# Delta's input through its 16 ranks: eight column-tiled products, a ScalarE copy and one fp32 product, in a Mamba block between two feed-forward blocks

## The chip, the cores and the metric

The kernel runs on one core of a Trainium2 chip. The metric is the device time of one execution in microseconds (us). TensorE (PE) multiplies, VectorE (DVE), ScalarE (ACT) and GpSimd (POOL) do the elementwise work, and SyncE (SP) issues most of the DMAs. The engines run their own instruction streams in order and meet at semaphores.

## What is computed

The input is 2 sequences of 2048 tokens of 256 numbers. Three layers follow one another, each on a layer-normed input and added back: a gated feed-forward block (hidden width 768, weights stored as integers), a Mamba block (inner width 512, 128 states), and the same feed-forward block again. The change lies in the Mamba block:

```
xz = x @ in_proj_w.T                 # x_in (512), z (512)
xc = causal_conv4(x_in) + conv_b     # per channel
ssm = xc @ x_proj_w.T                # 16 + 128 + 128 columns
dt_r, Bm, _ = split(ssm, [16, 144])
delta = clip(softplus(dt_r @ dt_proj_w.T + dt_proj_b), 0.001, 0.1)
A_bar = exp(delta * A);  B_bar = (A_bar - 1) / A * Bm
h[t] = A_bar[t] * h[t-1] + B_bar[t]
y = h @ C_proj_w.T + xc * D
out = (y * silu(z)) @ out_proj_w.T
```

Delta is a 128-wide quantity that comes from a 16-wide one (`dt_r`).

## The kernel before

**Tiles and halves.** A tile is 512 tokens of one sequence. The two sequences alternate: there are eight *halves* h = 0 to 7, and half h works on the Mamba block (part B) of one tile while it does the first feed-forward block (part A) of the tile that comes next and the second feed-forward block (part C) of the tile that has just left. Half 0 is the start (no C; it is woven with the preparation of the weights), halves 1 to 6 are alike, half 7 has no A, and a last C follows it alone. Activations are laid out with channels on partitions and 512 tokens along the free axis, so that most products are 128x128 weights against 128x512.

**Products.** Operands in half precision come as a high and a low part: for an fp32 accuracy product, three matmuls per 128 input channels (high x high, low weight x high, high weight x low). `ix`/`iz` are the in-projection, `xp0` and `xp1` the products that give delta's input and Bm, `cp` the state-to-channel product, `out` the out-projection, `gate`/`up`/`down` the feed-forward block. For `xp0` the kernel before folds `dt_proj_w @ x_proj_w[0:16]` once, in the preparation (`fill dt0`, a 16-row fp32 product, then `fill t0`, which transposes it), so that `xp0` is a 128-wide product like `xp1`: 12 matmuls each.

**Order and banks.** PE's order is written out by hand: `FIRST` for the preparation and half 0, `ORDER` for halves 1 to 6, `FINAL` for the rest. The order of ACT, DVE and POOL is that of their `half()` functions. Products go to a ring of four PSUM banks `q`: a product waits for whoever read the product four places earlier (`READER`). `down` and `out` use two other banks (`dp`).

**The way of delta.** `xp0` fills a bank; DVE adds the bias (`delta_in`, tile `sp`); ACT loads another function table and takes exp and log (`softplus_exp`, `softplus_log`); DVE clips (`dl`); ACT does `decay_relu` and `decay_exp` and loads the Silu table back; DVE runs a short series, multiplies, adds Bm (`input_in`, an ACT copy of `xp1`'s bank into `bm`) and scans (`hs`). `cp0` waits for the scan.

In halves 1 to 6 ACT comes to this after `split_hi`, two copies of the next A input (`xs<-xn`); the second one waits for DVE's `normalize(g, "A", (2, 3))`, which stands behind `hidden(g, "C", (4, 5))`, the reader of `up5`. In PE's order `up5` is just ahead of `xp0`.

Of the kernel before, what the change touches and what calls it, by code (L numbers as in the profile page):

```python
# [24 lines left out]
P = 128  # L25
# [11 lines left out]
TAPS = 4  # L37
EPS = 1e-5
# [19 lines left out]
def has(part, h):  # L58
# [54 lines left out]
def plan():  # L113
# [10 lines left out]
    for what, part, h in (*FIRST, *middle, *FINAL):  # L124
# [17 lines left out]
        elif what[:-1] == "xp":  # L142
            reader[take("ring", what + part, h)] = ("pc", h + 1) if what == "xp0" else ("bm", h + 1)
        elif what[:-1] in ("ix", "iz", "cp"):
            reader[take("ring", what + part, h)] = (what[:-1], IC * h + int(what[-1]) + 1)
# [48 lines left out]
def macaron(nc, x, in_w, conv_w, conv_b, xp_w, dt_w, dt_b, a_log, d_skip, c_w, out_w, wg, wu, wd, out):  # L194
    with ExitStack() as ctx:
# [53 lines left out]
        WXH = [sb(f"wxh{n}", [P, IC, N], F16) for n in range(2)]  # L249
        WXL = [sb(f"wxl{n}", [P, IC, N], F16) for n in range(2)]  # L250
# [37 lines left out]
        DTN = sb("dtn", [P, RANK])  # L288
        XPD = DL[0:RANK, :]
        DTT = DA[0:RANK, 0:N]  # L290
# [11 lines left out]
        NTS = SZ[0][:, 3, :]  # L302
# [24 lines left out]
        dtt_ready = sem("dtt_ready")  # L327
        small = sem("small")
# [34 lines left out]
        def _(sp):  # L363
# [8 lines left out]
            sp.dma_start(XPD, xp_w[0:RANK, :]).then_inc(ld["dt"], 16)  # L372
            sp.dma_start(DTN[:, :], dt_w).then_inc(ld["dt"], 16)
# [137 lines left out]
        def _(act):  # L511
# [21 lines left out]
            def fill(what):  # L533
# [15 lines left out]
                elif w in "xt":  # L549
                    act.activation(WXH[int(w == "t")][:, :, :].rearrange("p k n -> p (k n)"), bank[:, :], ACT.Copy)\  # L550
# [6 lines left out]
            def copy_rank():  # L557
                act.wait_ge(dt_turned, 1)
                act.activation(DTT, tp[0][0:RANK, 0:N], ACT.Copy).then_inc(dtt_ready, 1)

            def scale_x(n):
# [4 lines left out]
                else:  # L566
                    act.activation(NTS, filled("dt0")[:, :], ACT.Copy, scale=XRS[:, 1:2]).then_inc(w_act, 1)
# [70 lines left out]

            def softplus_exp(g):
                if g.h == 0:  # L640
                    act.wait_ge(unscale_ready, 1)
                act.wait_ge(pc_ready, g.index(1))
                act.activation(SP[:, :], SP[:, :], ACT.Exp, scale=XRI[:, 1:2]).then_inc(ep_ready, 1)
# [5 lines left out]
            def decay_relu(g):  # L649
                if g.h == 0:  # L650
                    act.wait_ge(const_ready, 3)
# [8 lines left out]
            def input_in(g):  # L660
                bank, uses = g.bank("xp1")
# [3 lines left out]
            def half(g):  # L665
# [47 lines left out]
                if B:  # L713
                    act.preload_act_table_set("natural_log_exp_and_others")
# [7 lines left out]
                if B:  # L722
                    input_in(g)
                if A and g.h > 0:
# [82 lines left out]
            silu_z(start, (2,))  # L807
            act.preload_act_table_set("natural_log_exp_and_others")
# [5 lines left out]
            gate(start, "A", (4,))  # L814
            input_in(start)
            gate(start, "A", (5,))
# [32 lines left out]
            hidden_high(late, "C", (4, 5))  # L849
            act.preload_act_table_set("natural_log_exp_and_others")  # L850
# [5 lines left out]
            input_in(late)  # L856
# [11 lines left out]
        def _(dve):  # L868
# [109 lines left out]
            def delta_in(g):  # L978

                bank, uses = g.bank("xp0")  # L980
# [172 lines left out]
            def x_proj_low(n):  # L1153
# [3 lines left out]
                high, low = (w[n][:, :, :].rearrange("p k n -> p (k n)") for w in (WXH, WXL))  # L1157
                dve.tensor_tensor(low, q[at % RING][:, :], high, ALU.subtract).then_inc(w_dve, 1)
# [28 lines left out]
            def x_proj_scale(n):  # L1187
# [4 lines left out]
                else:  # L1192
                    at = NUMBER["ring", "dt0", -1]
# [521 lines left out]
```

## Time and profile before

| | |
|---|---|
| time, 3 runs | 528.2, 530.04, 530.41 us; median 530.04 |
| the profiled execution | 528.34 us, of which 526.5 are its span |
| PE busy | 495.4 us |
| DVE, ACT, POOL busy | 415.4, 279.3, 235.7 us |
| one middle half (start of `xp0` to the next one) | 58.8 us (177.70 to 236.53) |

The span runs from the first to the last instruction; 1.84 us lie around it. A matmul's duration in the trace overlaps that of the next, so the pace of PE is read from the starts. "Idle before" is the time in which an engine had nothing running before an instruction, and after the arrow stands what it waited for.

### The profile page before, as it was taken

To read this page: it belongs to the slowest core of one execution; us is meant where nothing else is said; L and a number is where in the kernel's file an instruction comes from. 1 tells how busy PE (TensorE), PEld (TensorE's weight loads), DVE (VectorE), ACT (ScalarE), POOL (GpSimd) and SP (SyncE) were. 2 spreads that over 40 slices of the span, in tenths; PEclk is the share of its full clock that TensorE was granted. 3 is DMA by queue.
4 is the path that set the end of the run, shared out by engine and by line. 5 is a ranking of instruction groups with operands and counts; after the bars stand their busy time and mean duration, and the time that the engine had idled before them with its cause. 6 is when DMAs were issued, how large, how long until landed. Compare 5 with 4: busy or idle time off the path is not lost.

```text
span 526.5 us, 7720 instructions
## 1 busy us (share of the span) xinstructions
PE 495.4 (94%) x2657; PEld 292.6 (56%) x2657; DVE 415.4 (79%) x841; ACT 279.3 (53%) x472; POOL 235.7 (45%) x216
## 2 busy tenths in 40 slices
PE   2789988999999999999999999999999999999686
PEld 2346436646584457646574556646584557645444
DVE  4888996897879977997879877997879877787442
ACT  5384871477408671577408671577408671575032
POOL 1232237164733737163733735163733737163422
PEclk9898999999999999999999999999999999999979
DMA  8401000002020022003020112002020011000001
GB/s 294 130 0 43 2 0 2 0 2 42 21 61 2 9 34 81 1 1 42 23 60 1 20 23 81 1 2 41 24 60 1 18 26 42 1 1 21 20 1 42
DMA packets 27240, 16.84 MB, mean 32 GB/s; under 512 B 15264, under 2 KB 26528, under 8 KB 27184
## 3 DMA queue, kind: packets, MB, share of 16 engines
q1 hardware_dynamic: 26368, 15.26, 11.3%
q8 instruction: 40, 0.66, 0.5%
q10 hardware_dynamic: 816, 0.79, 0.5%
q14 instruction: 16, 0.13, 0.1%
HBM read 8.71 MB, written 4.19 MB: 24 GB/s over the span
## 4 chain that ended last, share of the span: by engine, by line
PE 81%; DVE 10%; ACT 3%; issue 3%; DMA 1%; POOL 1%; POOLq 0%; SPq 0%; ACTq 0%; DVEq 0%
PE q L1579 53%; PE dp L1579 25%; PE tp L1484 3%; DVE xc L968 1%; DMA hh<-in_L_ffn_w_gate_dram 1%; DVE h L943 1%; DVE xn L911 1%; POOL hl L432 1%; DVE hs L1025 1%; ACT xc L572 1%; DVE x L954 1%; DVE st_A L883 1%; DVE wmx L1063 0%; ACT sg L596 0%; DVE xl L920 0%
## 5 line engine op out<-in xcount | busy, mean ns | idle before, releaser
L432 POOL TENSOR_TENSOR hl<-h,hh 128x512 f16<-128x512 f32 x96 | 122.3, 1288 | 102.1 <-ACT hh L604 101.4
L943 DVE SCALAR_TENSOR_TENSOR h<-sg,hsm,q 128x512 f32<-128x512 f32 x96 | 70.5, 741 | 33.6 <-PE q L1579 21.4
L968 DVE SCALAR_TENSOR_TENSOR xc<-xi,cw,xc 128x512 f32<-128x512 f32 x96 | 87.1, 922 | 5.0 <-ACT xi L622 4.5
L578 ACT ACTIVATE xh<-tp 128x512 f16<-128x512 f32 x36 | 19.9, 609 | 113.2 <-PE tp L1484 113.2
L596 ACT ACTIVATE sg<-q 128x512 f32<-128x512 f32 x96 | 56.7, 591 | 36.7 <-PE q L1579 36.7
L604 ACT ACTIVATE hh<-h 128x512 f16<-128x512 f32 x96 | 60.1, 628 | 28.5 <-DVE h L943 28.2
L439 POOL TENSOR_TENSOR xcl<-xc,xch 128x512 f16<-128x512 f32 x32 | 40.6, 1278 | 51.7 <-ACT xch L629 51.7
L1579 PE MATMUL dp<-wo,yu 128*128 128x256 f32 x256 | 58.5, 380 | 1.5 <-POOL yu L447 1.5
L1579 PE MATMUL dp<-wd,hl 128*128 128x256 bf16 x384 | 53.4, 275 | 1.7 <-POOL hl L432 1.7
L1579 PE MATMUL dp<-wd,hh 128*128 128x256 bf16 x384 | 53.5, 276 | 0.9 <-ACT hh L604 0.9
L1579 PEld LDWEIGHTS dp<-wo,yu 128*128 128x128 f32 x256 | 47.2, 190 | 9.0 <-POOL yu L447 2.7
L1579 PEld LDWEIGHTS dp<-wd,hh 128*128 128x128 f16 x384 | 37.9, 99 | 12.9 <-issue 4.6
L447 POOL TENSOR_TENSOR yu<-yu,sz 128x512 f32<-128x512 f32 x32 | 39.6, 1268 | 8.8 <-DVE yu L1039 8.6
L1579 PEld LDWEIGHTS dp<-wd,hl 128*128 128x128 f16 x384 | 37.8, 99 | 7.1 <-issue 2.6
L1579 PE MATMUL q<-xh,wg 128*128 128x512 f16 x120 | 37.0, 391 | 3.8 <-DVE xl L920 3.1
L614 ACT ACTIVATE xc<-q,cb,rw 128x512 f32<-128x512 f32 x32 | 24.9, 779 | 28.9 <-PE q L1579 28.8
L1579 PE MATMUL q<-xl,wih 128*128 128x512 f16 x128 | 38.2, 379 | 0.0
L1579 PE MATMUL q<-xh,wih 128*128 128x512 f16 x128 | 38.1, 379 | 0.0
L1579 PE MATMUL q<-xh,wil 128*128 128x512 f16 x128 | 38.1, 379 | 0.0
L1579 PE MATMUL q<-xl,wg 128*128 128x512 f16 x120 | 37.2, 391 | 0.0
L1579 PE MATMUL q<-xt,wu 128*128 128x512 f16 x144 | 37.0, 379 | 0.0
L1579 PE MATMUL q<-xt,wg 128*128 128x512 f16 x144 | 37.0, 379 | 0.0
(169 smaller groups left out, 845.1 us busy)
## 6 DMA issues: line engine op xcount, KB each, us to landing
xpre<-in_L_attn_x_dram SPq DMA_DIRECT2D x8, 512.0 KB, 4.6
out_dram<-x SPq DMA_DIRECT2D x16, 256.0 KB, 2.1
xc<-in_L_attn_in_proj_w_dram SPq DMA_DIRECT2D x1, 1024.0 KB, 11.2
hl<-in_L_ffn_w_up_dram ACTq DMA_DIRECT2D x3, 256.0 KB, 6.3
hh<-in_L_ffn_w_gate_dram SPq DMA_DIRECT2D x3, 256.0 KB, 6.9
hh<-in_L_ffn_w_down_dram SPq DMA_DIRECT2D x1, 768.0 KB, 8.5
yu<-n_L_attn_out_proj_w_dram SPq DMA_DIRECT2D x1, 512.0 KB, 3.8
yu<-in_L_attn_x_proj_w_dram SPq DMA_DIRECT2D x1, 256.0 KB, 11.4
```

The costliest lines, as they stand in the source:

```text
L432: pool.tensor_tensor(HL[g.f][:, c, :], H[:, j, :], HH[g.f][:, c, :], ALU.subtract)\
L439: pool.tensor_tensor(XCL[:, m, :], XC[g.b][:, m, :], XCH[:, m, :], ALU.subtract)\
L447: pool.tensor_tensor(YU[g.b][:, m, :], YU[g.b][:, m, :], SZ[g.b][:, m, :], ALU.mult)\
L572: act.activation(NIS[:, c, :], NI[:, c, :], ACT.Copy, scale=RSC[:, c:c + 1]).then_inc(in_scaled, 1)
L578: act.activation(XH[g.f][:, kc, :], tp[kc][:, :], ACT.Copy, scale=XS).then_inc(t_hi[kc], 1)
L596: act.activation(SG[:, (first + c) % 2, :], q[bank][:, :], ACT.Silu, scale=QUANT / XS)\
L604: act.activation(HH[g.f][:, c, :], H[:, (first + c) % 3, :], ACT.Copy).then_inc(hh_ready, 1)
L614: act.activation(XC[g.b][:, m, :], q[bank][:, :], ACT.Identity, bias=CB[:, m:m + 1], scale=RW3[:, m:m + 1]).then_inc(xc_begun, 1)
L943: dve.scalar_tensor_tensor(out=H[:, first % 3, :], in0=SG[:, first % 2, :], scalar=HSM[:, c:c + 1], in1=q[bank][:, :], op0=ALU.mult, op1=A ...
L968: dve.scalar_tensor_tensor(out=XC[s][:, m, :], in0=XI[s][:, m, k:k + TILE], scalar=CW[:, m, k:k + 1], in1=XC[s][:, m, :], op0=ALU.mult, op ...
L1484: return pe.transpose(dst, src, IDN[:, :] if ident is None else ident)
L1579: ins = pe.matmul(out, w, a, start=(at == 0), stop=(at == len(terms) - 1))
```

## The change

Delta's input is no longer folded. `xp0` becomes the product with the 16 ranks: the high and the low half of the 16 weight columns lie side by side in `WR` (32 columns), and each of the four blocks of 128 channels goes to its own 32 partitions of the bank, first with the high part of `xc`, then with the low one: eight matmuls in four column tiles. A ScalarE copy (`rank_in`, into `RK`, which is the tile `ser`) brings the bank to SBUF, and a new fp32 product `xd0` of 128x128 weights `WDT` (eight copies of `dt_proj_w` transposed, one for each 16 rows, scaled) sums the eight pieces and gives delta's input. `xd0` stands behind `xp1` in the three orders. `input_in` moves to stand behind `rank_in`, ahead of the table load. In the preparation `fill dt0` goes, `fill t0` shrinks to 16 columns for each block, and two small loads become sixteen.

```diff
+COPIES = P // RANK
...
 ORDER = (("iz0", "B"), ("ix0", "B"), ("ix1", "B"), ("ix2", "B"), ("turn0", "C"), ("iz1", "B"), ("turn1", "C"),
...
-         ("up4", "C"), ("gate5", "C"), ("up5", "C"), ("xp0", "B"), ("xp1", "B"), ("down00", "C"),
+         ("up4", "C"), ("gate5", "C"), ("up5", "C"), ("xp0", "B"), ("xp1", "B"), ("xd0", "B"), ("down00", "C"),
...
-            sp.dma_start(XPD, xp_w[0:RANK, :]).then_inc(ld["dt"], 16)
-            sp.dma_start(DTN[:, :], dt_w).then_inc(ld["dt"], 16)
+            for j in range(COPIES):
+                sp.dma_start(XPD[RANK * j:RANK * (j + 1), :], xp_w[0:RANK, :]).then_inc(ld["dt"], 16)
+                sp.dma_start(DTN[:, RANK * j:RANK * (j + 1)], dt_w).then_inc(ld["dt"], 16)
...
+            def rank_in(g):
+                bank, uses = g.bank("xp0")
+                act.wait_ge(q_full[bank], uses)
+                wait(act, ssm_step, SSM_STEPS * g.index())
+                act.activation(RK[:, :], q[bank][:, :], ACT.Copy).then_inc(rk_ready, 1)
...
                 if A and g.h > 0:
                     split_hi(g, (1,))
                 if B:
+                    rank_in(g)
+                    input_in(g)
                     act.preload_act_table_set("natural_log_exp_and_others")
                     softplus_exp(g)
...
                     gate(g, "A", (0,))
-                if B:
-                    input_in(g)
-                if A and g.h > 0:
                     hidden_high(g, "A", (0,))
...
             silu_z(start, (2,))
+            rank_in(start)
+            input_in(start)
             act.preload_act_table_set("natural_log_exp_and_others")
...
-            gate(start, "A", (4,))
-            input_in(start)
-            gate(start, "A", (5,))
+            gate(start, "A", (4, 5))
...
             hidden_high(late, "C", (4, 5))
+            rank_in(late)
+            input_in(late)
             act.preload_act_table_set("natural_log_exp_and_others")
...
             table(ACT.Silu, 4)
-            input_in(late)
...
-                bank, uses = g.bank("xp0")
+                bank, uses = g.bank("xd0")
                 dve.wait_ge(q_full[bank], uses)
                 dve.tensor_scalar(SP[:, :], q[bank][:, :], DTB[:, 0:1], 0.0, ALU.add, ALU.min)\
...
+                dve.wait_ge(dtt_ready, 1)
+                dve.tensor_scalar(WDT[:, :], WDT[:, :], XRI[:, 1:2], None, ALU.mult).then_inc(wdt_ready, 1)
...
-                if w == "dt":
-                    ins = pe.matmul(q[at % RING][:, :], DTT, XPD, start=True, stop=True)
...
+            def rank_proj(g):
+                who, count = g.before("xp0")
+                pe.wait_ge(readers[who], count)
+                bank = g.bank("xp0")[0]
+                for low in range(2):
+                    for m in range(IC):
+                        pe.wait_ge((xch_ready, xcl_ready)[low], IC * g.index() + m + 1)
+                        ins = pe.matmul(q[bank][2 * RANK * m:2 * RANK * (m + 1), :], WR[:, m, :],
+                                        (XCL if low else XCH)[:, m, :], start=low == 0, stop=low == 1)
+                ins.then_inc(q_full[bank], 1)
+
+            def dt_proj(g):
+                if g.h == 0:
+                    pe.wait_ge(wdt_ready, 1)
+                pe.wait_ge(rk_ready, g.index(1))
+                product(g, "xd0", "B", [(WDT[:, :], RK[:, :])])
```

`variance(...)` gets its default argument written out, which changes no instruction.

The order on ACT in half 1, from the two copies of the A input on (`xs<-xn` is `split_hi`, `hh<-h` is `hidden_high`, `sp` are the softplus steps, `ex` the decay steps). Before:

```order
L586 ACTIVATE xs<-xn 128x512 [waits xn_ready]
L604 ACTIVATE hh<-h 128x512 [waits h_ready]
L586 ACTIVATE xs<-xn 128x512 [waits xn_ready]
L714 ACT_TABLE_LOAD
L643 ACTIVATE sp<-sp,xri 128x512 [waits pc_ready]
L647 ACTIVATE sp<-sp,one 128x512 [waits ep_ready]
```

And of the change:

```order
L597 ACTIVATE xs<-xn 128x512 [waits xn_ready]
L615 ACTIVATE hh<-h 128x512 [waits h_ready]
L597 ACTIVATE xs<-xn 128x512 [waits xn_ready]
L655 ACTIVATE ser<-q 128x512 [waits ssm_step,q_full1]
L679 ACTIVATE bm<-q,ia 128x512 [waits q_full2]
L732 ACT_TABLE_LOAD
L659 ACTIVATE sp<-sp 128x512 [waits pc_ready]
```

The copy `rank_in` (`ser<-q`) and `input_in` (`bm<-q,ia`) stand between the second `xs` copy and the table load.

The order on PE in half 1, at the end of `xp1` (`dp<-wd,hh` is the first matmul of `down00` of part C). Before:

```order
L1579 MATMUL q<-xch,wxh 128x512
L1579 MATMUL q<-xch,wxl 128x512
L1579 MATMUL q<-xcl,wxh 128x512
L1579 MATMUL dp<-wd,hh 128x256 [waits hh_ready,res_done]
L1579 MATMUL dp<-wd,hh 128x256 [waits hh_ready] x5
```

And of the change:

```order
L1601 MATMUL q<-xch,wxh 128x512
L1601 MATMUL q<-xch,wxl 128x512
L1601 MATMUL q<-xcl,wxh 128x512
L1601 MATMUL q<-ser,wdt 128x512 [waits sg_ready,rk_ready]
L1601 MATMUL dp<-wd,hh 128x256 [waits hh_ready,res_done]
```

`xd0` (`q<-ser,wdt`) stands between them and waits for the copy (`rk_ready`).

The order on PE in half 0, from the end of `xp1` on: the first matmuls of `gate5`, `iz3`, `up4` and `up5`, each with what it waits for. Before:

```order
L1579 MATMUL q<-xcl,wxh 128x512
L1579 MATMUL q<-xh,wg 128x512 [waits pc_ready]
...
L1579 MATMUL q<-xh,wih 128x512 [waits h_ready]
...
L1579 MATMUL q<-xh,wu 128x512 [waits sg_ready]
...
L1579 MATMUL q<-xh,wu 128x512 [waits bm_ready]
```

And of the change:

```order
L1601 MATMUL q<-xcl,wxh 128x512
L1601 MATMUL q<-ser,wdt 128x512 [waits rk_ready,wdt_ready]
L1601 MATMUL q<-xh,wg 128x512 [waits h_ready]
...
L1601 MATMUL q<-xh,wih 128x512 [waits sg_ready]
...
L1601 MATMUL q<-xh,wu 128x512 [waits bm_ready]
```

`xd0` takes a bank of the ring, so every wait moves up by one product: `gate5` now waits for the reader of `up3` (`h_ready`, DVE's `hidden` of chunk 3, which stands behind `delta_in`), and `iz3` for the reader of `gate4` (`sg_ready`, an ACT instruction that stands behind the whole softplus and decay block).

## Rows read from the trace of the kernel before

**Rows 1.** The page's busy times.

```profile
PE 495.4 (94%) x2657; PEld 292.6 (56%) x2657; DVE 415.4 (79%) x841; ACT 279.3 (53%) x472; POOL 235.7 (45%) x216
```

**Rows 2.** The chain that ended last, half 2: start, us, what.

```profile
183.04 5.24 PE dp L1579 x48
```

**Rows 3.** PE in order of time, half 2: xp0, xp1, down00 of C.

```profile
177.70 0.38 PE L1579 MATMUL q<-xch,wxh 128*128 128x512 f16 x1
...
182.88 0.82 PE L1579 MATMUL dp<-wd,hh 128*128 128x256 bf16 x6
```

**Rows 4.** ACT in order of time, half 2: second split_hi to softplus.

```profile
181.82 0.63 ACT L586 ACTIVATE xs<-xn 128x512 f16<-128x512 f32 x1 [1.75 <-DVE xn L911]
182.47 1.28 ACT L714 ACT_TABLE_LOAD   x1
184.06 0.72 ACT L643 ACTIVATE sp<-sp,xri 128x512 f32<-128x512 f32 x1 [0.30 <-DVE sp L982]
```

**Rows 5.** DVE in order of time, half 2: normalize of A's blocks 2, 3.

```profile
179.28 2.51 DVE L911 TENSOR_SCALAR xn<-xpre,mv_A,rs_A 128x256 f32<-128x256 f32 x2
```

**Rows 6.** Groups by line and form: ACT's fp32 copy of a bank; normalize of C.

```profile
L553 ACT ACTIVATE wc<-q 128x512 f32<-128x512 f32 x1 | 0.6, 605 | 0.0
...
L911 DVE TENSOR_SCALAR xn<-x,mv_C,rs_C 128x256 f32<-128x256 f32 x32 | 12.1, 406 | 1.0 <-POOL rs_C L420 1.0
```

**Rows 7.** PE, half 2: four fp32 products of 128x512 (two matmuls each).

```profile
198.48 3.60 PE L1579 MATMUL q<-hs,wc 128*128 128x512 f32 x8
201.91 0.82 PE L1579 MATMUL dp<-wd,hh 128*128 128x256 bf16 x6
```

**Rows 8.** Half 6, in order of time: xp0's first matmul; second split_hi.

```profile
414.13 0.38 PE L1579 MATMUL q<-xch,wxh 128*128 128x512 f16 x1
...
418.25 0.63 ACT L586 ACTIVATE xs<-xn 128x512 f16<-128x512 f32 x1 [1.74 <-DVE xn L911]
```

**Rows 9.** PE, half 0: end of xp0, gate5, cp0, the last matmul of down00.

```profile
69.30 0.39 PE L1579 MATMUL q<-xcl,wxh 128*128 128x512 f16 x1 [0.63 <-POOL xcl L439]
...
73.84 0.59 PE L1579 MATMUL q<-xh,wg 128*128 128x512 f16 x2
...
79.58 2.84 PE L1579 MATMUL q<-hs,wc 128*128 128x512 f32 x6 [0.78 <-DVE hs L1025]
...
84.58 0.28 PE L1579 MATMUL dp<-wd,hl 128*128 128x256 bf16 x1 [0.96 <-POOL hl L432]
```

**Rows 10.** ACT, half 0: first softplus step; gate4's Silu; input_in.

```profile
71.34 0.72 ACT L643 ACTIVATE sp<-sp,xri 128x512 f32<-128x512 f32 x1 [1.46 <-DVE sp L982]
...
76.27 0.57 ACT L596 ACTIVATE sg<-q 128x512 f32<-128x512 f32 x1
76.75 0.66 ACT L663 ACTIVATE bm<-q,ia 128x512 f32<-128x512 f32 x1
```

**Rows 11.** Half 7, in order of time, PE, DVE, ACT, PE.

```profile
475.34 0.38 PE L1579 MATMUL q<-xcl,wxh 128*128 128x512 f16 x1
...
475.75 0.75 DVE L982 TENSOR_SCALAR sp<-q,dtb 128x512 f32<-128x512 f32 x1 [1.13 <-PE q L1579]
...
476.60 0.72 ACT L643 ACTIVATE sp<-sp,xri 128x512 f32<-128x512 f32 x1
...
484.52 3.70 PE L1579 MATMUL q<-hs,wc 128*128 128x512 f32 x8 [0.98 <-DVE hs L1025]
```

**Rows 12.** Stretches: us, busy of PE, PEld, DVE, ACT, POOL, granted clock, DMA.

```profile
39.00:43.00 4.00, 4.00 (x19) 2.23 (x18) 2.82 (x16) 3.07 (x6) 2.75 (x3) 0.57 0.02 6
...
498.00:501.00 3.00, 0.00 (x0) 0.00 (x0) 2.37 (x12) 0.00 (x0) 1.34 (x2) 0.86 0.00 0
```

**Rows 13.** SP's last small load before C's; DVE's first use of them.

```profile
15.28 0.43 SPq L378 DMA_DIRECT2D al<-in_L_attn_A_log_dram  x1
...
30.95 0.16 DVE L1163 TENSOR_REDUCE xcb<-cw 128x4 f32<-128x16 f32 x1
```

**Rows 14.** PE in the preparation: fill dt0.

```profile
38.55 1.25 PE L1515 MATMUL q<-dl,da 16*128 16x512 f32 x2 [0.21 <-DVE wil L1150]
```

More of the change, by code:

```diff
@@ L142, in plan @@
         elif what[:-1] == "xp":
-            reader[take("ring", what + part, h)] = ("pc", h + 1) if what == "xp0" else ("bm", h + 1)
+            reader[take("ring", what + part, h)] = ("rk", h + 1) if what == "xp0" else ("bm", h + 1)
+        elif what[:-1] == "xd":
+            reader[take("ring", what + part, h)] = ("pc", h + 1)
         elif what[:-1] in ("ix", "iz", "cp"):
@@ L248, in macaron @@
         WIL = sb("wil", [P, KD, 2 * INNER], F16)
-        WXH = [sb(f"wxh{n}", [P, IC, N], F16) for n in range(2)]
-        WXL = [sb(f"wxl{n}", [P, IC, N], F16) for n in range(2)]
+        WXH = sb("wxh", [P, IC, N], F16)
+        WXL = sb("wxl", [P, IC, N], F16)
+        WR = sb("wr", [P, IC, 2 * RANK], F16)
+        WDT = sb("wdt", [P, N])
         WC = sb("wc", [P, INNER])
@@ L566, in scale_x @@
                 else:
-                    act.activation(NTS, filled("dt0")[:, :], ACT.Copy, scale=XRS[:, 1:2]).then_inc(w_act, 1)
+                    act.activation(XPS, XPD[0:RANK, :], ACT.Copy, scale=XRS[0:RANK, 1:2]).then_inc(rank_scaled, 1)
             def scale_row(c):
@@ L1192, in x_proj_scale @@
                 else:
-                    at = NUMBER["ring", "dt0", -1]
-                    dve.wait_ge(q_full[at % RING], at // RING + 1)
-                    rows = q[at % RING][:, :]
+                    dve.wait_ge(ld["dt"], 32 * COPIES)
+                    rows = XPD
                 at, to = (a[:, n:n + 1] for a in (XRM, XRS))
@@ L1352, in _ @@
             weight_rows("g", 2)
-            variance(before, "A")
+            variance(before, "A", (0, 1))
             weight_rows("u", 2)
@@ L1363, in _ @@
             flags[0] = flag_value(0)
-            variance(start, "A")
+            variance(start, "A", (0, 1))
             further_parts(0)
@@ L1393, in _ @@
             stats(before, "Bnext", (2, 3))
-            variance(before, "Bnext")
+            variance(before, "Bnext", (0, 1))
             hidden(start, "A", (0,))
@@ L1425, in _ @@
             stats(start, "Bnext", (2, 3))
-            variance(start, "Bnext")
+            variance(start, "Bnext", (0, 1))
             carry(start)
@@ L1471, in _ @@
             stats(last, "C", (2, 3))
-            variance(last, "C")
+            variance(last, "C", (0, 1))
             normalize(last, "C", (0, 1, 2, 3))
@@ L1554, in turn_norm @@
                 if part == 0:
+                    if k == "Bnext" and g.h < 0:
+                        pe.wait_ge(dtt_ready, 1)
                     for kc in range(KD):
@@ L1611, in in_proj, with b_proj @@
                         waits=split_waits(g, "Bnext", 2 * KD, back=1) if m == 0 else {})
-            def x_proj(g, n):
-                ready = {3 * m + 2 * low: ((xch_ready, xcl_ready)[low], IC * g.index() + m + 1)
-                         for m in range(IC) for low in range(2)}
-                product(g, f"xp{n}", "B", [(w[1 - n][:, m, :], part[:, m, :]) for m in range(IC)
-                                           for w, part in ((WXH, XCH), (WXL, XCH), (WXH, XCL))],
-                        waits={} if n else ready)
+            def rank_proj(g):
[9 more added lines that the diff above has]
+            def dt_proj(g):
+                if g.h == 0:
+                    pe.wait_ge(wdt_ready, 1)
+                pe.wait_ge(rk_ready, g.index(1))
+                product(g, "xd0", "B", [(WDT[:, :], RK[:, :])])
+            def b_proj(g):
+                product(g, "xp1", "B", [(w[:, m, :], part[:, m, :]) for m in range(IC)
+                                        for w, part in ((WXH, XCH), (WXL, XCH), (WXH, XCL))])
             def c_proj(g, m):
@@ L1673, in do @@
                     in_proj(g, what)
-                elif what[:-1] == "xp":
-                    x_proj(g, int(what[-1]))
+                elif what == "xp0":
+                    rank_proj(g)
+                elif what == "xp1":
+                    b_proj(g)
+                elif what == "xd0":
+                    dt_proj(g)
                 elif what[:-1] == "cp":
```

65 lines of the change are left out of this document (36 added, 29 removed), and 6 rows, old and new, of tables (FINAL, FIRST).

## The prediction

> **What bounds the kernel now.** I read the busy times first: PE is busy 94% of the span [rows 1], so any time on PE counts unless it falls into one of PE's few waits. The chain that ended last says the same for the middle: in half 2 it is PE for long stretches, of which one is shown [rows 2]. Then PE in order of time where the change cuts in: from `xp0` to `down00` there is no wait, 24 matmuls in 182.88 - 177.70 = 5.18 us, 0.216 each [rows 3]. Last, what ACT, DVE and the start and end of the kernel look like, because there PE does wait: for the scan at `cp0` in halves 0 and 7 (0.78 and 0.98), and once for POOL in `down00` of half 0 (0.96) [rows 9, 11].
>
> **Halves 1 to 6.** On PE alone the change is a gain. Twelve matmuls (2.59 us) go. Eight come: at worst one after the other, 8 x 0.216 = 1.73, at best four side by side, 0.43. One fp32 product of 128x512 comes: 3.43 us for four (198.48 to 201.91) is 0.86 [rows 7]. Sum on PE: between 0.00 and -1.30 per half.
>
> But `xd0` waits for `rank_in`, and PE runs in order, so `down00` and all behind it wait too. `rank_in` is an ACT instruction behind the second `split_hi`, which starts at 181.82 and lets the table load start at 182.47 [rows 4]; it can't come sooner, since it waits for DVE's two normalizations, 2.51 us from 179.28 [rows 5]. ACT starts the next one about 0.1 before the last ends (76.27 + 0.57 against 76.75) [rows 10], so the copy runs from 182.35, 0.60 us (an ACT copy of an fp32 bank) [rows 6], to 182.95. A product that had to wait starts some 0.05 later and takes 0.1 more (3.70 for the four that waited, 3.60 for those that didn't) [rows 7, 11]: `xd0` ends at 183.00 + 0.97 = 183.97. Before, `down00` began at 182.88. That is **+1.09 per half**, and how fast the eight matmuls are doesn't enter: `xp1` ends at 180.7 or 182.0, ahead of the copy either way. The offset is the same in all of these halves: 181.82 - 177.70 = 4.12 in half 2, 418.25 - 414.13 = 4.12 in half 6 [rows 3, 4, 8]. PE has no slack to give it back, so 6 x 1.09 = **+6.5**.
>
> What else moves there: ACT takes `rank_in` and `input_in` ahead of the table load, so the load ends at 182.95 + 0.6 + 1.28 = 184.8, and the first softplus step goes from 184.06 to 184.9, as delta's input comes at 184.0 + 0.2 and DVE takes 0.75 for it. That is less than PE's 1.09, so the scan isn't later for PE than before. `split_lo`'s second half stands behind `delta_in` on DVE and the DMA transpose of the A input behind it: +0.9, again less than PE's own delay. These are priced at nothing; without this cover each would cost at most what exceeds 1.09.
>
> **Half 0.** Here the order of before gave softplus its input early: `xp0` ends at 69.5, `up3`, `gate4` and `xp1` stand between, and the first softplus step starts at 71.34 [rows 9, 10]. Now the ACT stream waits for `xp1` (in `input_in`) before it loads the table. `xp0` still ends when POOL's last `xcl` is there; I take 0.4 off, as DVE's subtraction of the folded weights ahead of it shrinks to an eighth. So `xp1` ends at 73.84 - 0.4 = 73.44 [rows 9], its bank is read 0.2 later, `input_in` 0.67, table 1.28: softplus at 75.64, **+4.3**. The copy and `xd0` (74.3, then `delta_in` to 75.2) fit in front of that. The same +4.3 holds for the Silu of `gate4` (76.27 to 80.6) [rows 10]. A little comes back, since before the multiplication by Bm waited 0.35 for `input_in`: the scan, and after it `hidden`, `hl` and the last matmul of `down00` (84.58) [rows 9], are 3.95 later. PE meanwhile stands still: `gate5` waits for `hidden` of chunk 3 until 76.6, `iz3` for the Silu until 81.2, 3.7 us without work.
>
> What a stop like that does to the clock: PE was idle before 501.0, and in 498 to 501 the granted clock was 0.86, that is it had already gone from 2.4 to 1.2 GHz; in 39 to 43 it was 0.57 with PE busy all the time, so such a dip cost 0.43 x 4 = 1.7 us of work [rows 12]. With the dip, `iz3`, `up4`, `up5` take 4.7 instead of 3.0, PE reaches `cp0` at 85.9 and the end of `down00` at 89.6, where the others would let it go on at 88.5: **+1.0**. Half 0: 3.95 + 1.0 = **+5.0**.
>
> **Half 7.** No A, so no `split_hi`; the copy comes at 475.2 and PE doesn't wait for it. But ACT's table load, which ended in time for softplus at 476.60 [rows 11], now stands behind `input_in`, and that behind `xp1`. `xp1` ends at 473.0 + 1.73 + 2.59 = 477.3 if the eight run one by one; a bank is read 0.41 after its last matmul starts (475.34 to 475.75) [rows 11]: 477.5, then 0.68 and 1.28: softplus at 479.5, **+2.9**. If four run side by side it is 478.4, **+1.8**. `cp0` waits for the scan already, so all of it counts. No row shows column tiles; I take one by one, the pace of every row. PE then stands 4 us before `cp0` and the clock dips; POOL's multiplications behind `cp` hide part of it. Bounds 0.3 and 2.1, I take **+1.0**.
> The Trainium skill holds that column tiles overlap (TensorE: Matmul & The Clock Gate, Part 3: three column tiles of width 32 were 2.38 times as fast); no row here shows it, and by it the sum would be 1.1 lower.
>
> **Preparation.** `fill dt0` (1.25) goes [rows 14], but `down00` waits for POOL's `hl` right behind it and DVE sets the pace; **-0.2**. Fourteen more DMA issues of 0.43 delay the small loads by 6 us: the last goes from 15.28 to 21.3, and DVE first wants them at 30.95 [rows 13]. Nothing. With that cover gone it would be 6.
>
> **Sum.** 6.5 + 5.0 + 2.9 + 1.0 - 0.2 = 15.2 on 528.34, the profiled execution: 543.5. Two of the three runs before are 1.7 to 2.1 above it, the median is 530.04; I place mine between, at 544.5.
>
> **Rivals.**
> (a) *The copy is early, and the change is a gain.* If the second `split_hi` came sooner, `xd0` would follow `xp1` at once. The point is a copy that ends before `xp1` does, at 180.7 to 182.0 instead of 182.95. DVE's two normalizations take 1.25 each here and 0.41 where POOL isn't at work [rows 5, 6]; at that pace `split_hi` starts at 180.1 and the copy ends at 181.3. Then the six halves give up to -1.3 each, -7.8, and if halves 0 and 7 cost nothing either, 8 x -1.3 = -10.4: 518. Against it: nothing in the change moves POOL's `hl` off that stretch. 0.04. With the costs of halves 0 and 7 it ends at 527 to 532: 0.06.
> (b) *The clock dips in halves 1 to 6 as well.* With four tiles side by side PE stands from 180.7 to 183.0. A dip costs up to 1.7; in three to six halves that is 5 to 10 more: 549 to 555. Against it: PE works on either side of that stop, where it did nothing at all from 498 to 501 [rows 12]. 0.15.
> (c) *PE hides more than I think* (no dip in halves 0 and 7, tiles side by side, `split_hi` a little earlier): 532 to 538. 0.09.
> (d) *The change does what it says only on paper*: column tiles run slower than full ones, since PE has to empty between shapes. The row where nothing overlaps is the duration of one matmul, 0.38 [rows 3]: 8 x 0.38 = 3.0, `xp1` ends at 183.3, +0.4 more in each of the six and +1.3 in half 7, total 547 to 548. Inside my range.
> The Trainium skill has this as a rule (TensorEngine Tiling (Array Packing), Key Properties: a change of tiling mode drains the array); the wait for the copy would hide such a drain in six halves, so by that page too the sum stays.
> The forecast itself, 538 to 549: 0.66.
>
> **Range and chances.** 536 to 551 leaves out (a) and most of (b). A difference under 0.5% can't be told from none here. Faster 0.04, same 0.05, slower 0.91.
>
> **What the profile after would show.** Right: in halves 1 to 6 a PE wait of 1 to 2.5 us before the fp32 matmul of `ser` and `wdt`, put down to ACT's `ser` copy, which starts with no gap behind the second `xs`; a period of 59.9 us instead of 58.8; in half 0 PE waits for `h` before `gate5` and for `sg` before `iz3`, some 6 us together, and a granted clock under 1 after it; in half 7 softplus 1.8 to 2.9 later against `xp0`. Wrong: the copy ends before `xp1` does, or the period is under 58.8; or a PE wait at `gate0` of A for the DMA transpose, or at `cp0` in the middle halves, which would mean that a side chain lost its cover.

## The result and the profile after

The changed kernel takes 547.82 us (median of four runs, 546.63 to 550.33); the kernel before, beside it, 530.03 (four runs). The ratio is 1.034 with an interval of 1.031 to 1.037: slower. The profiled execution took 546.63 us, its span is 544.6, 18.1 more than before.

Of the changed kernel, first the page's busy times [rows 1], then three lines of the list of waits (engine, operation and line that waited, the one waited for, us in total, times, longest):

```profile
PE 496.2 (91%) x2639; PEld 289.6 (53%) x2639; DVE 417.5 (77%) x841; ACT 282.9 (52%) x480; POOL 236.3 (43%) x216
...
PE q L1643 <- POOL xcl L448: 5.9, 8, 0.8
...
PE q L1601 <- ACT ser L655: 2.9, 6, 0.5
...
PE q L1601 <- ACT sg L607: 3.4, 1, 3.4
```

PE is busy for about as long as before (496.2 against 495.4) and the span is longer: 17.3 of the 18.1 us are time in which PE has nothing running. Six waits are for the copy (`ser`), one in each of halves 1 to 6. Eight are for POOL's `xcl`, one in each of the eight halves, at the last of the narrow matmuls; the prediction doesn't have those.

PE, ACT and POOL in order of time in half 2, around `xp0` and behind it, of the changed kernel (answers to [rows 3, 4]):

```profile
184.82 2.28 POOL L448 TENSOR_TENSOR xcl<-xc,xch 128x512 f16<-128x512 f32 x2 [1.36 <-ACT xch L640]
185.00 0.59 PE L1601 MATMUL q<-xl,wu 128*128 128x512 f16 x2
185.15 0.63 ACT L640 ACTIVATE xch<-xc 128x512 f16<-128x512 f32 x1
185.53 0.69 PE L1643 MATMUL q<-xch,wr 128*32 128x512 f16 x4
185.83 0.59 PE L1643 MATMUL q<-xcl,wr 128*32 128x512 f16 x3
187.15 0.39 PE L1643 MATMUL q<-xcl,wr 128*32 128x512 f16 x1 [0.72 <-POOL xcl L448]
187.47 0.39 PE L1601 MATMUL q<-xch,wxh 128*128 128x512 f16 x1
...
189.56 0.63 ACT L597 ACTIVATE xs<-xn 128x512 f16<-128x512 f32 x1 [1.74 <-DVE xn L927]
190.09 0.58 ACT L655 ACTIVATE ser<-q 128x512 f32<-128x512 f32 x1
190.57 0.68 ACT L679 ACTIVATE bm<-q,ia 128x512 f32<-128x512 f32 x1
...
190.72 1.12 PE L1601 MATMUL q<-ser,wdt 128*128 128x512 f32 x2 [0.49 <-ACT ser L655]
191.69 0.82 PE L1601 MATMUL dp<-wd,hh 128*128 128x256 bf16 x6
```

Read it from the bottom: `down00` starts 6.16 us after `xp0` (191.69 - 185.53), before it was 5.18. It starts when `xd0` is done, `xd0` when the copy is done, and the copy stands with no gap behind the second `xs`. PE's wait is printed as 0.49, though `xp1`'s last matmul starts at 189.85 and could have been followed at 190.07: a wait is counted from the modelled end of the matmul before, so starts tell the loss (0.65), the bracket doesn't. The narrow matmuls start as soon as their operands are there. Three of the high group start within 0.01; the fourth starts at 185.83, 0.05 after ACT's last `xch` copy ends (185.15 + 0.63), a wait that the row doesn't print, and the first low ones start with it: the column tiles run side by side. And still `xp1` begins only 1.94 after `xp0`, since the last low matmul waits for POOL, whose last two `xcl` end at 187.10.

Half 0 of the changed kernel, PE and ACT (answers to [rows 9, 10]):

```profile
69.27 0.39 PE L1643 MATMUL q<-xch,wr 128*32 128x512 f16 x1 [2.06 <-ACT xch L640]
...
70.51 0.39 PE L1643 MATMUL q<-xcl,wr 128*32 128x512 f16 x1 [0.83 <-POOL xcl L448]
...
75.42 0.69 ACT L679 ACTIVATE bm<-q,ia 128x512 f32<-128x512 f32 x1 [3.89 <-PE q L1601]
76.12 1.28 ACT L825 ACT_TABLE_LOAD   x1
77.42 0.63 ACT L659 ACTIVATE sp<-sp 128x512 f32<-128x512 f32 x1
...
78.40 0.60 PE L1601 MATMUL q<-xh,wg 128*128 128x512 f16 x2 [2.23 <-DVE h L959]
...
82.82 1.04 PE L1601 MATMUL q<-xh,wih 128*128 128x512 f16 x2 [3.38 <-ACT sg L607]
...
87.48 1.02 PE L1601 MATMUL q<-hs,wc 128*128 128x512 f32 x2
```

ACT waits for `xp1` in `input_in`, loads the table after that, and softplus comes at 77.42 instead of 71.34; PE stands 2.23 us at `gate5` and 3.38 at `iz3`. After the stand at `iz3` a matmul pair takes 1.04 instead of 0.60. The stretches show it in the clock (granted clock: the third number from the end):

```profile
71.00:75.00 4.00, 4.00 (x20) 1.82 (x19) 0.57 (x4) 0.53 (x1) 1.70 (x2) 1.00 0.00 0
...
79.00:83.00 4.00, 0.62 (x4) 0.13 (x2) 3.79 (x7) 3.64 (x6) 0.00 (x0) 0.54 0.00 0
83.00:87.00 4.00, 4.00 (x12) 1.45 (x11) 3.93 (x5) 1.97 (x4) 3.17 (x2) 0.61 0.00 0
```

From 79 to 83 PE worked 0.62 us and the granted clock was 0.54, near the lower level of 1.2 GHz (0.50); from 83 to 87 it was 0.61 with PE at work all the time, and in the four us behind that 1.00 again.

Half 7 of the changed kernel, PE and ACT (answers to [rows 11]):

```profile
488.39 0.39 PE L1643 MATMUL q<-xcl,wr 128*32 128x512 f16 x1 [0.72 <-POOL xcl L448]
...
491.52 0.69 ACT L679 ACTIVATE bm<-q,ia 128x512 f32<-128x512 f32 x1 [2.02 <-PE q L1601]
492.22 1.28 ACT L867 ACT_TABLE_LOAD   x1
493.52 0.63 ACT L659 ACTIVATE sp<-sp 128x512 f32<-128x512 f32 x1
...
501.34 5.40 PE L1601 MATMUL q<-hs,wc 128*128 128x512 f32 x8 [3.77 <-DVE hs L1041]
```

`xp0` starts at 486.77 here. The scan is waited for 3.77 instead of 0.98, and the eight matmuls behind it take 5.40 instead of 3.70, as the clock is down again (0.57 from 502 to 506).

**The ledger.** The first `xp0` matmul of a half is a mark that every kernel has. Four stretches between such marks, in us, read from PE's order of time (the last ends with the span):

| kernel | start to half 0 | half 0 | halves 1-6 | shortest of them | half 7 to end |
|---|---|---|---|---|---|
| before | 65.17 | 53.70 | 354.10 | 58.83 | 53.6 |
| before, second trace | 65.96 | 53.73 | 354.52 | 58.83 | 54.2 |
| changed | 66.82 | 58.81 | 361.15 | 59.90 | 57.8 |
| changed, second trace | 66.70 | 60.66 | 361.58 | 59.89 | 58.0 |
| changed, third trace | 66.51 | 60.78 | 361.36 | 59.90 | 57.8 |

In every one of these traces half 4 is 1.1 to 1.5 longer than the shortest half: there PE waits for the scan at `cp0` (0.46 in the kernel before). That is no work of the change.

The experiments below are told in these stretches, with one trace for each kernel unless the text says more. Ratios are to the kernel before, run beside each. Of each edit the diff is against the changed kernel, unless the kernel before is named.

### The profile page after: what moved, and what is told of

Read it like the earlier page. It is cut to its first block, busy times and chain, and to the rows that moved or that the text cites. A ratio compares the mean times of both kernels' runs of the same rounds, so it can differ in the third digit from the quotient of the medians.

```text
span 544.6 us, 7719 instructions
## 1 busy us (share of the span) xinstructions
PE 496.2 (91%) x2639; PEld 289.6 (53%) x2639; DVE 417.5 (77%) x841; ACT 282.9 (52%) x480; POOL 236.3 (43%) x216
## 3 DMA queue, kind: packets, MB, share of 16 engines
q1 hardware_dynamic: 27600, 15.55, 10.6%
## 4 chain that ended last, share of the span: by engine, by line
PE 75%; DVE 11%; ACT 5%; issue 4%; DMA 2%; POOL 2%; POOLq 0%; SPq 0%; ACTq 0%; DVEq 0%
PE q L1601 49%; PE dp L1601 23%; DVE xn L927 3%; PE tp L1505 3%; DVE xc L984 2%; DMA hh<-in_L_ffn_w_gate_dram 1%; DMA xt<-xs 1%; POOL hl L441 1%; DVE h L959 1%; ACT ser L655 1%; POOL xcl L448 1%; DVE hs L1041 1%; DVE x L970 1%; ACT xc L583 1%; ACT sg L607 0%
## 5 line engine op out<-in xcount | busy, mean ns | idle before, releaser
L456 POOL TENSOR_TENSOR yu<-yu,sz 128x512 f32<-128x512 f32 x32 | 39.8, 1273 | 12.6 <-DVE yu L1055 12.6
L1601 PE MATMUL q<-xh,wu 128*128 128x512 f16 x120 | 37.4, 395 | 0.0
```

Source lines behind the costliest of these rows:

```text
L456: pool.tensor_tensor(YU[g.b][:, m, :], YU[g.b][:, m, :], SZ[g.b][:, m, :], ALU.mult)\
L1601: ins = pe.matmul(out, w, a, start=(at == 0), stop=(at == len(terms) - 1))
```

## The experiments

**The copy ahead of the second `split_hi`** (halves 1 to 6):

```diff
-                if A and g.h > 0:
-                    split_hi(g, (1,))
                 if B:
                     rank_in(g)
+                if A and g.h > 0:
+                    split_hi(g, (1,))
+                if B:
                     input_in(g)
```

> The change, with one ACT instruction moved in halves 1 to 6: the copy of the ranks (rank_in) stands ahead of the second copy of the A input (split_hi) and no longer behind it. My theory: PE's wait before xd0 in these halves is the queue on ACT, so it goes, xd0 follows xp1 at once, and down00 starts 0.76 us earlier in each half: 6 x -0.76 = -4.6, some 542 to 543 where the change has 546.6 to 548. Rival: the middle halves are slower because of the column tiles and the extra fp32 product themselves (PE is emptied, the matmuls are slower), and the wait would only turn up elsewhere: no change, 546 to 548.

545.66 us (four runs), ratio 1.030 (1.025 to 1.036). The time alone is inside the noise of the changed kernel's, the trace isn't: the shortest period is 59.14 instead of 59.90, halves 1 to 6 take 356.9 instead of 361.1 to 361.6. Half 0 and the end, which the edit doesn't touch, took 60.6 and 59.0 in this trace. ACT and PE in half 2 of this kernel:

```profile
187.17 0.60 ACT L655 ACTIVATE ser<-q 128x512 f32<-128x512 f32 x1
...
189.53 1.02 PE L1602 MATMUL q<-ser,wdt 128*128 128x512 f32 x2
190.39 0.82 PE L1602 MATMUL dp<-wd,hh 128*128 128x256 bf16 x6
```

The copy starts 2.4 us before `xd0`, which no longer waits. So the place of the copy is worth 0.76 per half, and 0.31 of the 1.07 stay. What is left is time on PE itself, POOL's wait included: `xp0` now fills 1.94 instead of 2.59 (12 x 0.216), `xd0` adds 0.86, and the step from the full matmuls of `up5` to the first narrow one costs 0.09 (185.53 - 185.00 = 0.52 for the last two of `up5` in the rows of the changed kernel above, 0.43 at the usual pace): 0.30 of the 0.31.

**Without the low half of `xp0`.** The four matmuls of `WR` with `XCL` are left out, so delta's input lacks the low part of `xc`. (`xp1`, which uses the low parts too, then waits for them itself; no such wait shows in halves 1 to 6.)

```diff
-                for low in range(2):
-                    for m in range(IC):
+                for m in range(IC):
```

> The change, with the low half of xp0 left out (the four matmuls with the low part of xc, so delta is less exact; work is left out), and with them PE's 0.72 us wait for POOL's last xcl. My theory: in halves 1 to 6 nothing changes, since xd0 waits for the copy anyway (the wait before xd0 grows from 0.49 to about 1.4 us); in halves 0 and 7 together about 1.5 us go: -1.5. Rival (PE's own work and POOL's wait set the pace): 6 x 0.9 more, -7.

545.33 us, ratio 1.028 (1.022 to 1.034). PE in half 2 of this kernel, `xp0` starting at 183.86:

```profile
183.86 0.69 PE L1642 MATMUL q<-xch,wr 128*32 128x512 f16 x4
...
189.06 1.13 PE L1601 MATMUL q<-ser,wdt 128*128 128x512 f32 x2 [1.81 <-ACT ser L655]
```

Four matmuls and POOL's wait are gone, the wait for the copy grows from 0.49 to 1.81 (1.4 was expected), and the shortest period stays at 59.90. In halves 1 to 6 what `xp0` costs on PE does not matter in the changed kernel. In this trace these halves even took 362.8, as half 4 was 62.39 long. Against half 1, its matmuls fall behind at three places: 0.50 at the first one on the transposed A input (`xt`, 316.52), 1.1 at `cp0` for the scan, as in every kernel, and 0.83 at 337.01, where `out` waits for DVE's residual sum, which itself waited 3.67 for an output store. Half 0 (57.5) and half 7 (56.6 to the end) are 1.2 to 1.3 shorter than in the first trace of the change: there the low half counts.

**The start in the order of before**: `xd0` right behind `up3`, `input_in` between `gate4` and `gate5` on ACT.

```diff
-         ("up3", "A", 0), ("gate4", "A", 0), ("xp1", "B", 0), ("xd0", "B", 0), ("gate5", "A", 0), ("iz3", "B", 0),
+         ("up3", "A", 0), ("xd0", "B", 0), ("gate4", "A", 0), ("xp1", "B", 0), ("gate5", "A", 0), ("iz3", "B", 0),
...
             rank_in(start)
-            input_in(start)
...
-            gate(start, "A", (4, 5))
+            gate(start, "A", (4,))
+            input_in(start)
+            gate(start, "A", (5,))
```

> The change, with half 0 put right alone: xd0 stands behind up3 and ahead of gate4 and xp1, and input_in stands between the Silu of gate4 and gate5 again. My theory: the cost of half 0 (about 5.3 us in the trace of the change) comes from the softplus chain starting behind xp1, from the ring waits that moved up, and from the clock dip of the stop; all but about 0.9 goes: -4.4, some 542 to 544, and the granted clock stays 1.0 from 79 to 88 us. Rival: the chain through ranks, copy and fp32 product is simply longer, and half 0 stays 3 us or more slower than before.

543.99 us (543.63 to 544.62), ratio 1.026 (1.021 to 1.031). Half 0 takes 55.5: 3.3 to 5.2 less than in the three traces of the change, 1.8 more than before. PE and ACT in half 0, and the clock behind it:

```profile
72.23 1.91 PE L1602 MATMUL q<-ser,wdt 128*128 128x512 f32 x2
...
75.04 0.63 ACT L659 ACTIVATE sp<-sp 128x512 f32<-128x512 f32 x1 [2.03 <-DVE sp L999]
```

```profile
71.00:75.00 4.00, 4.00 (x10) 1.59 (x10) 2.47 (x7) 1.88 (x2) 1.84 (x2) 0.57 0.00 0
```

The clock is worth nearly all of the 1.8: at 0.57 four us do the work of 2.3, and `xd0` takes 1.91 instead of 1.02. But that is a count; no run has this order without the fall, and softplus comes 8.06 behind `xp0` here, 6.17 before, part of which is the longer way of delta. Here the low clock comes at 71 to 75, ahead of the stands at `gate5` and `iz3`, which this kernel doesn't have. It comes after the stand in `xp0`, and the second and third trace of the changed kernel have it as well.

**The end in the order of before**: in half 7 `xd0` ahead of `xp1`, `input_in` behind the decay steps.

```diff
-         ("xp0", "B", 7), ("xp1", "B", 7), ("xd0", "B", 7),
+         ("xp0", "B", 7), ("xd0", "B", 7), ("xp1", "B", 7),
...
             rank_in(late)
-            input_in(late)
...
             table(ACT.Silu, 4)
+            input_in(late)
```

> The change, with half 7 put right alone: xd0 stands ahead of xp1 (PE waits about 0.8 us for the copy there), and input_in stands behind the decay steps again. My theory: the first softplus step comes 2.0 us earlier, the stop before cp0 is shorter and the clock dip in it smaller: -2.0 to -2.8, some 544 to 545.5. Rival: the end is longer for another reason (the dip comes anyway, or xp1's delay of the Bm copy takes over): under 1 us.

545.35 us, ratio 1.030 (1.026 to 1.035). From `xp0` (488.78) to the end it takes 54.9 instead of 57.8 to 58.0, 2.9 less; before it was 53.5 and 54.2. PE and ACT in half 7:

```profile
491.55 1.13 PE L1601 MATMUL q<-ser,wdt 128*128 128x512 f32 x2 [0.76 <-ACT ser L655]
...
493.50 0.63 ACT L659 ACTIVATE sp<-sp 128x512 f32<-128x512 f32 x1 [0.70 <-DVE sp L998]
...
501.33 3.70 PE L1601 MATMUL q<-hs,wc 128*128 128x512 f32 x8 [0.82 <-DVE hs L1041]
```

Softplus comes 4.72 behind `xp0`; in the changed kernel 6.75, before 3.64. With the stand at `cp0` down from 3.77 to 0.82 the clock stays up (1.00 from 486 to 514) and the eight matmuls take 3.70 again. These orders leave the longer way itself: product, copy, product, bias.

**All three orders together.**

> The three edits of order together: the copy ahead of split_hi, half 0 and half 7 put right; the arithmetic is that of the change. My theory: the effects add up, -4.6 - 4.4 - 2.4 = -11.4, some 536, still 6 us above the kernel before: 0.3 in each middle half (xp0 waits 0.72 for POOL's xcl), 0.9 in half 0, 1 to 2 in half 7, and the preparation. Rival: they overlap and give 8 or less.

534.80 us, ratio 1.009 (1.005 to 1.012). That is 13.0 us less than the changed kernel, or 12.6 when each is set against the kernel before beside it: of the 17.8 us some 13 are order, not work. The stretches: half 0 55.5, halves 1 to 6 357.2 (period 59.14), half 7 to the end 54.8. The three edits alone gave 2.2, 3.8 and 2.5 us by their medians, less than 13 in sum, but their intervals are 5 to 6 us wide. The stretches of the traces come near the sum: 4.2 + 3.3 to 5.3 + 3.1, that is 10.6 to 12.6.

**The low half inside `xp1`.** All three orders, and in halves 1 to 6 the four low matmuls of `xp0` in the middle of `xp1`, where POOL is done; `input_in` behind softplus.

```diff
+                for at, (w, a, m, low) in enumerate(terms):
+                    if at == 6 and 0 < g.h < LAST - 1:
+                        rank_proj(g, (1,))
...
-                    input_in(g)
                     act.preload_act_table_set("natural_log_exp_and_others")
                     softplus_exp(g)
                     softplus_log(g)
+                    input_in(g)
```

> All three edits of order, and besides: in halves 1 to 6 the low half of xp0 stands in the middle of xp1, so that PE doesn't wait for POOL's last xcl, and input_in stands behind the softplus log, so that the table load follows split_hi at once as before. My theory: a middle half is then 0.5 to 0.6 us shorter than before on PE, half of which the scan may take back at cp0: -1.5 to -3.3 in all, against +2 for halves 0 and 7: 528 to 531, no difference from before that can be told. Rival: every switch between column tiles and full tiles costs PE more than 0.1 us, or the longer way of delta holds cp0: 532 to 536.

531.25 us (twelve runs), ratio 1.0032 (1.0014 to 1.005). PE in half 2:

```profile
180.72 0.69 PE L1646 MATMUL q<-xch,wr 128*32 128x512 f16 x4
181.34 0.39 PE L1668 MATMUL q<-xch,wxh 128*128 128x512 f16 x1
...
182.74 0.40 PE L1646 MATMUL q<-xcl,wr 128*32 128x512 f16 x4
183.07 0.39 PE L1668 MATMUL q<-xch,wxh 128*128 128x512 f16 x1
...
184.38 1.02 PE L1603 MATMUL q<-ser,wdt 128*128 128x512 f32 x2
185.24 0.82 PE L1603 MATMUL dp<-wd,hh 128*128 128x256 bf16 x6
```

No wait is printed any more: `xp0`, `xp1` and `xd0` take 4.52 instead of 5.18, and the shortest period is 58.26, 0.57 under that of before. So the change can be a gain in halves 1 to 6, but a smaller one than the 1.30 that four tiles side by side seemed to give. Two things take 0.7 of it back. A group of four costs 0.43, twice the 0.22 of one full matmul, as the steps into narrow matmuls and out of them come to 0.09 and 0.11; there are two groups. And the high group takes 0.29 longer, because its fourth matmul still waits for ACT's last `xch`.

The six halves took 353.1, only 1.0 less than before instead of 3.4: three of them were 0.7 to 1.4 longer than the shortest (58.94, 59.58, 59.61), where before one was, by 1.1. Set against half 2 matmul by matmul, 1.1 of half 4 is the wait for the scan that every kernel has, and 0.4 of half 3 a wait for DVE's residual sum. The rest starts at the first matmul on the transposed A input: about 0.2 in each of halves 3 to 5 and 1.3 in half 6, where the wait is printed:

```profile
427.43 0.65 PE L1603 MATMUL q<-xt,wg 128*128 128x512 f16 x2 [1.13 <-DMA xt<-xs]
```

That is the side chain that I had named under "Wrong". It had lost its cover in half 6 of the changed kernel already (0.41 to 0.57 in the three traces), and it costs more once PE is fast. Half 0 (55.4) and the end (55.0) take 1.7 and 0.8 to 1.4 more than before, and the gain is eaten.

**The same again.**

> The interleaved kernel once more, beside the kernel with up3 ahead: 1.003 of the kernel before, as in its first run, with the fall of the clock at 71 to 75 and 55.4 us for half 0.

531.13 us (twelve runs), ratio 1.0026 (1.001 to 1.0041); half 0 55.46, halves 1 to 6 353.05, with 1.20 us of wait at the same place of half 6.

**`up3` ahead of `xp0` in half 0**, in the interleaved kernel.

```diff
-         ... ("up2", "A", 0), ("xp0", "B", 0), ("up3", "A", 0), ("xd0", "B", 0),
+         ... ("up2", "A", 0), ("up3", "A", 0), ("xp0", "B", 0), ("xd0", "B", 0),
```

> The interleaved kernel, and in half 0 the product up3 (four matmuls, 0.86 us) ahead of xp0 instead of behind it, so that it runs while xp0 would wait 2.06 us for the last xch. The waits of half 0 end as before; nothing is later. If the clock's fall at 71 to 75 comes from the long stand at xp0 (1.1 us of work in 67 to 71, against 2.6 in the kernel before), it is gone or shorter: half 0 lasts 53.7 to 54.3 us instead of 55.4, and the kernel is 1.2 to 1.7 us faster than the interleaved one, level with the kernel before. If it comes from somewhere else, half 0 stays at 55.4 and the time at that of the interleaved one (half 0's PE work is the same in sum).

531.32 us, ratio 1.0022 (1.0005 to 1.004), the same as the interleaved kernel beside it: a miss. PE in half 0 of this kernel, and its clock:

```profile
69.38 0.39 PE L1646 MATMUL q<-xch,wr 128*32 128x512 f16 x1 [1.20 <-ACT xch L640]
...
70.61 0.39 PE L1646 MATMUL q<-xcl,wr 128*32 128x512 f16 x1 [0.83 <-POOL xcl L448]
71.73 2.05 PE L1603 MATMUL q<-ser,wdt 128*128 128x512 f32 x2 [0.73 <-issue]
```

```profile
71.00:75.00 4.00, 3.27 (x6) 1.11 (x6) 2.80 (x7) 2.20 (x3) 1.78 (x2) 0.57 0.00 0
```

The stand at `xp0` shrank from 2.06 to 1.20 and PE worked 1.96 us in 67 to 71 instead of 1.11, but `up3` is missing behind it, and `xd0`, with nothing in front, stands 0.73 for its copy, which ran from 71.04 to 71.64 (the row says "issue"). I had moved the idle time, not removed it, so the run doesn't tell whether the stand makes the clock fall.

**The sixteen loads in the kernel before.** They go into two tiles that aren't yet in use; the product still reads one copy.

```diff
+            for j in range(8):
+                sp.dma_start(DL[RANK * j:RANK * (j + 1), :], xp_w[0:RANK, :]).then_inc(ld["dt"], 16)
+                sp.dma_start(BM[:, RANK * j:RANK * (j + 1)], dt_w).then_inc(ld["dt"], 16)
```

> The kernel before, with the sixteen small loads of the change in place of two. In the trace of the change the preparation is 1.3 us longer than before. My theory: that is not the loads but the phase of the clock in the first 20 us (the eight weight transposes at 14.1 us took 1.97 instead of 1.10): no difference, 528 to 531. Rival: fourteen more loads delay the first weights or what waits for the small loads: +1.3 or more, and the first gate matmul starts at 20.4 in place of 19.05.

530.26 us (ten runs), ratio 1.0009 (0.998 to 1.0038). The interval reaches from 1.1 us less to 2.0 us more, so it would also hold the 1.3 in question. First gate matmul at 19.87, `xp0` of half 0 at 66.35.

**The kernel before once more.**

> The kernel before once more, for its trace: how far the first 20 us and the clock in them move from one execution to the next. My theory for the 1.3 us of the preparation (clock phase) wants a spread of 0.5 to 1.5 us in the start of the first gate matmul among the traces of kernels whose first 20 us are alike; rival: it stays at 19.05 within 0.2 in this kernel and at 20.3 in all kernels with the sixteen loads.

530.28 us; first gate matmul at 19.21 instead of 19.05, `xp0` of half 0 at 65.96 instead of 65.17.

**The changed kernel twice more.**

> The changed kernel once more, for one more trace. If the 1.3 us by which its first gate matmul came later (20.36 against 19.05) belongs to the sixteen loads, it starts near 20.3 again; if it is the spread from one execution to the next, anywhere between 19.0 and 20.4. The waits behind the copy of the ranks, 0.49 in each of halves 1 to 6, and the softplus of half 0 six us later than before, should be there again.

> The same, a third trace: period of a middle half 59.9 us, and in half 0 a granted clock near 0.5 behind the wait for the Silu at iz3, as in the first trace.

548.73 and 548.35 us. First gate matmul at 20.24 and 19.57. The 0.49 before `xd0` and the period are there again. Half 0 takes 60.66 and 60.78, 1.9 more than in the first trace, and the stretches of the second trace say where:

```profile
67.00:71.00 4.00, 1.10 (x10) 0.37 (x8) 3.83 (x8) 1.39 (x3) 2.71 (x3) 1.00 0.00 0
71.00:75.00 4.00, 4.00 (x13) 1.45 (x11) 1.50 (x3) 0.41 (x1) 1.56 (x2) 0.58 0.00 0
...
83.00:87.00 4.00, 2.62 (x7) 0.95 (x8) 3.86 (x5) 2.83 (x6) 1.60 (x2) 0.50 0.00 0
```

The clock falls twice, at 71 to 75 and again from 79 on. A fall costs 0.42 x 4 = 1.7 us. The first trace had only the second fall; it is also the fastest of the six executions (546.63).

## Why the prediction was right

The forecast was 544.5 us in 536 to 551; 547.8 came. The sum was 543.5 against the profiled execution's 546.63, 3.1 too low. By its own terms, the first trace of the change against the first trace before (0.2 of the difference lie outside the spans):

| term | forecast | measured |
|---|---|---|
| halves 1 to 6 | +6.5 | +7.05 |
| half 0 | +5.0 | +5.11 (+6.9, +7.1 in the two others) |
| half 7 | +3.9 | +4.3 (+3.6 against the second trace before) |
| preparation | -0.2 | +1.65 (+0.9 against the second trace before) |

**Halves 1 to 6: the bound right.** Forecast 1.09 per half, measured 1.07. The copy stands behind the second `xs` without a gap, `xd0` starts 0.05 behind the copy's end and takes 0.97 (191.69 - 190.72). The two experiments that pull on its two ends show the cause: with the copy earlier 0.76 comes back, with four matmuls fewer nothing does. One sign missed: the wait before `xd0` was to be 1 to 2.5 us and is printed as 0.49 (0.65 by the starts). I had `xp1` end 3.0 to 4.3 behind the start of `xp0`; it ended 4.54 behind it (190.07 - 185.53), since `xp0` waits for what it reads. The copy, at 5.14, was still the later of the two, so the price stood. The other 0.6 of the term is half 6, which took 60.53 instead of 59.90: PE waited 0.41 at `gate0` of A for the DMA transpose. I had priced that chain at nothing, as 0.9 later against 1.09; in one half in six the cover didn't hold, in all three traces.

**Half 0: the waits right, the clock half right.** Softplus was put at 75.64; it came at 77.42, which is 75.77 less the 1.65 by which the whole half started later. The stands were to be "some 6 us together" and were 5.6. The fall of the clock behind them came. The one ahead of them, at 71 to 75, I didn't foresee; two of three traces have it, and it is the mis-sized step: the term should have been 5 to 7. That the first trace agrees to 0.1 is luck; it is the one without that fall. The likely source of the fall is a consequence of the narrow product. Before, the twelve matmuls of `xp0` filled the time in which ACT and POOL split `xc`: PE waited 0.80 and 0.63. The eight narrow ones leave waits of 2.06 and 0.83, and PE works 1.1 us in 67 to 71 instead of 2.6. None of the three traces with the full product (the kernel before twice and with sixteen loads) has a fall there, nor has the kernel without the low half, which stands 2.06 us at `xp0` too but works 2.1 us in that stretch; with the narrow product and its low half, all have it but the first of the changed kernel (nine of ten). That is a correlation: the attempt to take the stand away failed, and the cause of this fall stays open.

**Half 7: the right number by a wrong way.** I took the eight matmuls one after the other (1.73), which gave softplus +2.9; side by side it would have been +1.8. They ran side by side, and softplus came 3.11 later (6.75 behind `xp0` against 3.64). What fills the gap is the wait for `xcl`: from `xp0` to `xp1` 1.94 go by whatever the tiles do. The step "how fast the eight matmuls are" had left out what they read, ACT's `xch` and POOL's `xcl`. In halves 1 to 6 this wait was hidden by that for the copy; when the copy was early it became the bound, and only the interleaved kernel got rid of it. The clock's share was +1.2 (4.3 - 3.1), forecast 1.0.

With their operands ready, four tiles start within 0.02 us (182.74, 0.40 for all four, in the interleaved kernel). Going from full matmuls to narrow ones costs 0.09, and from narrow to full ones 0.10 (187.47 - 187.15 = 0.32 against 0.22), far from the 0.38 that rival (d) took for each matmul. The Trainium skill says that column tiles overlap (TensorE: Matmul & The Clock Gate, Part 3), which these rows bear out; the Trainium skill also says that a change of tiling mode drains the array (TensorEngine Tiling (Array Packing), Key Properties), of which no more than 0.09 on the way in and 0.10 on the way out is seen.

**Preparation: wrong.** Forecast -0.2, measured +1.65, of which 1.31 is there before the first gate matmul. The sixteen loads are not shown to cost it, nor to be free: in the kernel before, their time is the same within an interval that would also hold the 1.3. The first gate matmul starts at 19.05 and 19.21 in the two traces without them and anywhere from 18.98 to 20.36 in the twelve traces of kernels that have them, later than 19.21 in eleven. What goes with it is the pace of the first transposes: the eight at about 14 took 1.10 in both traces without the loads and in one with them (18.98), and 1.97 in the other eleven, with a granted clock printed as 1.00 from 13 to 17. A part of 0.33 is the change's own: PE waits that long for DVE's subtraction that makes the low half of `WR`, which stands behind the convolutions. Whether the rest is the spread of single executions or comes with the loads stays open.

**The rivals.** (a) was the mechanism of the first experiment, but not a gain even there: the period was still 0.31 above that of before, as the wait for `xcl` took its place. (b) did not come. A stretch of the changed kernel around `xd0` in half 2:

```profile
186.00:191.00 5.00, 3.78 (x18) 1.55 (x16) 4.65 (x4) 3.26 (x7) 4.54 (x4) 1.00 0.00 0
```

The granted clock is 1.00 there, and over all of 126 to 486 in each of the three traces. Of (c) the side-by-side tiles came, the rest didn't; (d) is refuted by the starts. That its 547 to 548 is the time that came is chance, and its own 0.4 per half was too much: with `xp1` ending at 183.3 the product behind it would not have waited, 183.3 + 0.86 = 184.2 against 183.97, 0.2 per half.

## What to carry over

Work that moves to a new engine pays at that engine's place in line, not at its duration: a copy of 0.6 us behind a `split_hi` that itself waits for another engine held each of six halves back by 1.07, of which 0.76 came back when it moved one place forward, while the matmuls saved on PE counted for nothing. When a product is made shorter, ask what it was covering: here it had filled the time in which its own operands were made. And before a change with a new dependency is judged, try the orders around it: some 13 of 17.8 us were order, though here even the best order ended 0.3% behind the kernel before.

## What the runs showed of the hardware

Matmuls of 32 columns in four column tiles last 0.39 us each as full ones do, but four start within 0.02 us when their operands are there (182.74, 0.40 for all four). Where a group was spread wider, the one that came late had waited: in half 2 of the changed kernel the fourth started 0.05 after ACT's last `xch`, in half 0 the last low one 0.83 later for POOL's `xcl`. So a group of four costs as much as two full matmuls (0.43 with both steps), not as one. A weight load of 32 columns takes 92 ns in the trace, one of 128 columns 98.

The clock's falls make identical executions differ: the three traces of the changed kernel differ by 1.9 us in half 0 by one fall more or less, half of the 3.7 by which its six times differ.
